# Last attention of a four-layer vision tower: order of the maxima, the results and the output projection within a step

## The reference, cut to what matters

```python
def gqa(x, wq, wk, wv, wo, n_kv):          # D_MODEL 128, N_HEADS 8, D_K 16
    B, S, _ = x.shape
    q = (x @ wq).reshape(B, S, N_HEADS, D_K).transpose(0, 2, 1, 3)
    k = (x @ wk).reshape(B, S, n_kv, D_K).transpose(0, 2, 1, 3)
    v = (x @ wv).reshape(B, S, n_kv, D_K).transpose(0, 2, 1, 3)
    k = jnp.repeat(k, N_HEADS // n_kv, axis=1)
    v = jnp.repeat(v, N_HEADS // n_kv, axis=1)
    scores = jnp.einsum('bhqd,bhkd->bhqk', q, k) / jnp.sqrt(jnp.float32(D_K))
    attn = jax.nn.softmax(scores, axis=-1)
    out = jnp.einsum('bhqk,bhkd->bhqd', attn, v)
    return out.transpose(0, 2, 1, 3).reshape(B, S, D_MODEL) @ wo

logits = jax.nn.relu(x.mean(axis=1) @ r_w1 + r_b1) @ r_w2 + r_b2
sel = jnp.argmax(jax.nn.softmax(logits, axis=-1), axis=-1)
for i, nkv in enumerate((8, 4, 1)):
    out = jnp.where((sel == i)[:, None, None], gqa(x, *params[i], nkv), out)
# x is the normalized h; the kernel's output is h + out
```

## Time and profile before

| what | us |
|---|---|
| median of 3 runs | 1234.58 |
| lowest and highest run | 1231.76, 1241.58 |
| the profiled execution's own time | 1236.1 |
| its span, first to last instruction | 1234.3 |
| PE busy (share of the span) | 1098.2 (89%) |
| DVE busy | 904.1 (73%) |
| ACT busy | 845.1 (68%) |
| POOL busy | 526.2 (43%) |

### The profile page before, as it was taken

How to read it: one execution, slowest core, us unless ns; L and a number is a source line. 1 busy time by engine, 2 the same in 40 slices (tenths; PEclk the granted TensorE clock), 3 DMA queues, 4 the chain that set the end, 5 groups by cost and what they waited for, 6 DMA issues and landing times. The chain is left out here.

```text
span 1234.3 us, 29279 instructions
## 1 busy us (share of the span) xinstructions
PE 1098.2 (89%) x8508; PEld 910.6 (74%) x8508; DVE 904.1 (73%) x2770; ACT 845.1 (68%) x2821; POOL 526.2 (43%) x885
## 2 busy tenths in 40 slices
PE   8999979999998999887388599998899899869996
PEld 5778857888887788776288477786678688657884
DVE  0488847999976889956565488886899788755774
ACT  1498858888885555557243378887788499846995
POOL 0379864444304278855252653323342011034552
PEclk9999989999999999988599689999999999959997
DMA  7300002322210000001522200000333100024441
GB/s 293 96 2 3 2 1 63 110 71 65 65 43 23 1 2 1 2 1 38 195 61 50 63 14 2 11 2 2 115 113 113 34 3 2 2 80 122 131 130 36
DMA packets 50824, 66.68 MB, mean 54 GB/s; under 512 B 8100, under 2 KB 30904, under 8 KB 50552
## 3 DMA queue, kind: packets, MB, share of 16 engines
q1 hardware_dynamic: 44552, 53.39, 14.2%
q0 software_dynamic: 4432, 6.59, 2.1%
q10 hardware_dynamic: 1696, 4.98, 1.0%
HBM read 58.32 MB, written 6.71 MB: 53 GB/s over the span
## 5 line engine op out<-in xcount | busy, mean ns | idle before, releaser
L495 DVE TENSOR_TENSOR f_parts<-T,f_parts 128x512 fp32r<-128x512 f32 (+1 forms) x240 | 181.7, 796 | 21.1 <-ACT f_parts L479 19.6
L471 ACT ACTIVATE T<-quad_bank,f_b1s 128x512 f32<-128x512 f32 (+1 forms) x240 | 150.5, 648 | 43.2 <-PE quad_bank L442 34.3
L442 PE MATMUL quad_bank<-XP,f_wp 128*128 128x512 f32 (+1 forms) x720 | 165.3, 373 | 1.1 <-ACT T L471 1.1
L442 PEld LDWEIGHTS quad_bank<-XP,f_wp 128*128 128x128 f32 x720 | 125.6, 188 | 26.4 <-ACT T L471 1.4
L479 ACT ACTIVATE f_parts<-T 128x512 fp32r<-128x512 f32 (+1 forms) x240 | 132.7, 593 | 0.0
L954 ACT ACTIVATE a_late<-quad_bank,a_shift 108x108 f32<-108x108 f32 x352 | 119.1, 363 | 2.7 <-DVE a_shift L1022 2.4
L455 PE MATMUL bank<-f_parts,f_wp 128*128 128x512 f32 (+1 forms) x480 | 116.7, 379 | 4.7 <-DVE XT L504 2.0
L455 PEld LDWEIGHTS bank<-f_parts,f_wp 128*128 128x128 f32 x480 | 85.4, 192 | 23.5 <-DVE a_late L524 2.8
L384 POOL TENSOR_TENSOR f_wp<-f_ws,const 128x512 fp32r<-128x512 f32 (+1 forms) x32 | 31.0, 968 | 122.3 <-DMA f_ws<-in_f_w 53.9
L954 ACT ACTIVATION_READ_ACCUMULATOR a_late<-quad_bank,a_shift 108x1 f32 x352 | 77.2, 219 | 0.0
L765 POOL TENSOR_TENSOR a_ve<-a_mv,const 108x1 f32<-108x1 f32 x44 | 8.3, 189 | 152.1 <-DVE a_mv L1079 152.0
(11 more groups left out here) (470 smaller groups left out, 3105.9 us busy)
## 6 DMA issues: line engine op xcount, KB each, us to landing
a_late<-f_gates SPq DMA_DIRECT2D x64, 256.0 KB, 3.2
a_wqk<-in_a_wqk SPq DMA_DIRECT2D x24, 256.0 KB, 2.5
f_ws<-in_f_w SPq DMA_DIRECT2D x16, 256.0 KB, 3.8
pats<-in_patches SPq DMA_DIRECT2D x5, 648.0 KB, 10.7
pats<-in_patches ACTq DMA_DIRECT2D x5, 648.0 KB, 14.8
a_late<-f_gates SPq DMA_DIRECT2D x16, 128.0 KB, 3.6
f_w1a<-in_f_w SPq DMA_DIRECT2D x1, 2048.0 KB, 11.4
f_w2a<-in_f_w SPq DMA_DIRECT2D x1, 2048.0 KB, 16.2
```

Of the source, the lines that this page charges most:

```text
L442: mm = pe.matmul(self.m.quad_bank[:, q % 4, 0:w], self.wp[0][:, e % 2, a, c * 128:(c + 1) * 128], self.xp[:, b, t0:t0 + w], start=((a, b) ...
L471: act.activation(self.full[:, q % 4, 0:w], self.m.quad_bank[:, q % 4, 0:w], self.func, bias=self.b1s[:, e * self.chunks + c:e * self.chunk ...
L495: dve.tensor_tensor(self.lo[:, q % self.ring, 0:w], self.full[:, q % 4, 0:w], self.hi[:, q % self.ring, 0:w], ALU.subtract).then_inc(self. ...
```

## The change

On TensorE, `probabilities(t - 2, par, 1)`, that is P1, moves from behind wo to ahead of it. On VectorE, recT and oT move from the end of step t (for group t-2) to step t+1 (there group t-3 of that step), where they stand between the two maxima: mx0, shift0, recT, oT, mx1, shift1. The waits and the operations themselves stay as they are.

```diff
@@ TensorE, step
                 if isinstance(t, int) and t == 2:
                     keep_busy(pe, m, obank, 3)
+                if on(t, 2):
+                    probabilities(t - 2, par, 1)
                 if on(t, 3):
                     g = t - 3
                     pe.wait_ge(o_done, g + 1)
...
                     pe.wait_ge(wo_loaded[q], landed(g, q))
                     pe.matmul(xbank[0:P, 0:D], oT[:, :], wo[:, q, :], start=True, stop=True).then_inc(y_psum, 1)
-                if on(t, 2):
-                    probabilities(t - 2, par, 1)
@@ VectorE, step
                 if on(t, 1):
                     maxima(t - 1, q, 0)
+                if on(t, 3):
+                    g = t - 3
+                    dve.wait_ge(o_psum, g + 1)
+                    at_least(dve, o_done, g)
+                    dve.tensor_copy(recT[:, :], z_at).then_inc(o_read, 1)
+                    dve.wait_ge(o_read, g + 1)
+                    at_least(dve, y_psum, g)
+                    dve.tensor_tensor(oT[:, :], o_at, recT[:, :], ALU.mult).then_inc(o_done, 1)
+                if on(t, 1):
                     maxima(t - 1, q, 1)
...
-                if on(t, 2):
-                    g = t - 2
-                    dve.wait_ge(o_psum, g + 1)
-                    at_least(dve, o_done, g)
-                    dve.tensor_copy(recT[:, :], z_at).then_inc(o_read, 1)
-                    dve.wait_ge(o_read, g + 1)
-                    at_least(dve, y_psum, g)
-                    dve.tensor_tensor(oT[:, :], o_at, recT[:, :], ALU.mult).then_inc(o_done, 1)
```

## The result

| | before | after |
|---|---|---|
| median of 20 runs, us | 1234.53 | 1240.71 |
| lowest and highest | 1228.32, 1241.58 | 1231.61, 1248.41 |
| ratio, 95% interval | | 1.0047 (1.003 to 1.0064) |
| profiled execution, its span | 1236.1, 1234.3 | 1246.6, 1244.8 |

What follows compares the result with a forecast made beforehand. PE was taken to bound the stage, with the order of work deciding. Loop +3.45, unrolled steps +0.65 and tail +1.2 sum to +5.3 us, giving a median of 1239.9 us, range 1234.5 to 1244.5.

Steps and rivals of the forecast that it cites:

- The point to see: Last attention, PE: wo stands exactly in the hole where P1 waits for ACT's pT0, and just covers that wait.
- E: Loop step behind the loop's branch; forecast hole ahead of P1 0.30 us, next S0 at 4.52.
- F: The other loop step, not behind the branch; forecast hole ahead of P1 0.26 us, its next S0 at 9.11.
- P1's wait: On PE, P1 starts 0.15 us behind pT0's end; lower end 0.05, which would make the whole change +3.3.
- A pair of 9.11: Two successive loop steps forecast at 9.11 us, for 8.665 before; loop +3.45 us.
- The ring: Cycle over PE and ACT: P1, wo, qk, v, v's copy, exps1, xT, pT0, P1; 4.48 us.
- part 2: DVE's recT and oT between the maxima: all fits barely, slack about 0 and 0.07 us, z at most 0.05 late.
- Rival C: Chance 0.20: DVE becomes the bound if the moved pair costs 0.2 us more; +7.7 us, 1242.3.
- Unrolled steps +0.65: The four unrolled steps t = 3 to 6 take 4.48 us each instead of 4.315, +0.65 us.
- Tail +1.2: At t = 24 wo stands behind P1, so h, recs, z and o come later at half clock: +1.2 us.
- Rival B: Chance 0.15: early maxima win, P1 finds pT0 ready at S1's end; faster, together -1.0 us, 1233.6.
- Rival D: Chance 0.02: PE's clock falls to half in the stage, with a hole each step; +60 us.

Runs made afterwards that it cites:

- exchanged banks: Changed kernel with P1 moved to x's PSUM bank, wo and v to P0's bank: ratio to before 1.002; the same with VectorE's old order: 0.9987.

## Why the prediction was right, and where it wasn't

**Sign, size and stage: right.** The stage's own loss is 4.03 us in the profiled executions. The median's +6.2 is above it, but the interval, from 3.7, holds it; what the rest is, beyond the scatter of the code ahead of the stage, stays open.

**"The point to see": right, and shown.** wo stood in the place of the hole. The hole of 0.30 in E came out as 0.30, that of 0.26 in F as 0.18; a filler in it costs 0.02 a step, and taking P1's wait away removes it.

**P1's wait, 0.15 taken with 0.05 as the lower end: right, with luck.** It is 0.15 where P1 does wait (1162.59 to 1162.74). But the row it was read from doesn't show it: in the kernel before P1 stands behind wo by wo's pitch of 0.30 to 0.31 in both steps, and in F that is 0.23 behind pT0's end. That it was 0.15 in E is a coincidence. The Trainium skill, "Advanced Engine Details and Errata", section Network/Comms, gives 50 to 100 ns for reading a semaphore; by that figure alone the hole in E would be 0.20 to 0.25, an estimate, and the trace shows 0.30.

**A pair of 9.11: measured 9.10, and that is luck, as errors cancel.** The two steps came out the other way round, E 4.59 for 4.52 and F 4.52 for 4.59. The step that failed is "I take P1 to wo as 0.37 and wo to qk as 0.31, each by its leader's pitch". The 0.31 was read where wo's weight load starts 0.01 ahead of its matmul (1172.61 and 1172.62 in the kernel before). In the kernel with TensorE's part alone it starts 0.09 ahead, qk follows wo by 0.22, and P1's own pitch is 0.39. The ring is shorter by 0.07 a step or so, and that kernel's pair is 9.00. The other 0.10 comes from part 2.

**Part 2, "all fits, barely": wrong.** oT's end was forecast at S0 + 2.22 and came at 2.21. But "in time for wo at 2.40" left out wo's weight load, which starts 0.23 behind oT's end, at S0 + 2.44. The matmul is at 2.45 then, 0.02 later behind P1 than without VectorE's part, but qk is 0.30 behind it and not 0.22. recs comes at S0 + 3.49 and z at 3.87, both 0.02 late. So VectorE's order adds 0.89 us to the loop on top of the hole. Rival C was right that the moved pair costs, and wrong on the way: in the changed kernel S0 stands 0.51 behind o, its pitch, and 0.15 behind the qk add's end, where 0.12 was forecast, and with exchanged banks it is the same; the ring closes over recs, z and o. Without the hole, VectorE's path is the bound and costs 2.41 by itself. Why the load starts 0.23 behind oT here and 0.14 in the kernel with exchanged banks stays open.

**Unrolled steps +0.65: measured +0.20.** They were charged by the loop's ring, 4.48 a step, and take 4.36. The same shorter pitch behind wo, 0.22 for 0.31, is most of the difference; the hole there is 0.13 to 0.15.

**Tail +1.2: the mechanism was right, the size 0.99 at half clock and 0.66 at full.** wo lasts 0.64 there, not the 0.76 taken, and z to o is 0.34, not 0.41. In the profiled execution little of it shows in the end time: from S0 at t = 23 to the last h it is 10.69 us against 10.36. The clock fell some 2 us of work later in that run (v, z and o of t = 23 ran at full clock), so that P1 of t = 24 stands 5.69 behind S0 of t = 23 and not 6.35, which gives 0.66 of the 0.99 back. That is luck of the run, as other executions with the same order show the full clock to o and beyond.

**The sum.** The parts in the profiled executions are 3.50, 0.20 and 0.33, together 4.03, for 3.45, 0.65 and 1.2. The ends of the range don't follow from its own recipe (1237.9 - 3 is 1234.9, 1242.3 + 3 is 1245.3); the measured time lies well inside either way.

**Rival B: refuted.** mx0 comes 0.22 earlier with respect to S0 (0.76 for 0.98) and nothing is gained: with VectorE's part alone the pair is 9.83, and with the exchanged banks, where P1 waits for nothing, the new VectorE order is 2.41 slower than the old. **Rival D** did not happen in the changed kernel, and it did in the one with VectorE's part alone. The Trainium skill's rule ("TensorE: Matmul & The Clock Gate", section Part 4: PE-mode transpose) that turning doesn't count as busy for the clock gate is neither shown nor refuted: the clock stayed at 1.00 with ten turned blocks and a hole in each step, and it fell behind a larger hole in a kernel with the same turned blocks.

## What to carry to other kernels

An instruction whose inputs are long ready can be what hides the wait of the one behind it. Before two neighbours on an in-order engine are exchanged, write down for each when its inputs are ready and when its slot comes; if the one that moves forward is ready only 0.1 us behind its new slot, the loss can be paid in each step, as the 0.18 and 0.30 were here. A result that another engine needs at once (oT for wo) should not be put behind work with slack; and where a place on an engine is idle anyway, as VectorE's between the qk add and mx0, the work that stands there is free, and moving it out delays what it is put ahead of: mx1 started 0.22 us later (S0 + 2.13 for 1.91).

## What was not expected of the hardware

- A wait against a constant passed 0.05 us behind the event (oT's end 1133.91, wo 1133.96). The same wait in the loop, with two more waits on register values behind it, passed 0.22 behind it (1183.65, 1183.87). In the kernel with exchanged banks, with as many waits on register values, it was 0.14 (1161.80, 1161.94), so their number alone doesn't set it. Writing the loop out cut the change's cost from 3.50 to 0.92 us. The runs don't separate the register waits from the other differences of the two forms.
- Turned blocks start 0.15 behind the event they wait for, in the loop and written out alike: P1 behind pT0, z behind recs (1164.42, 1164.57).
- How early a matmul's weight load can start shows in the pitch of the next matmul: wo to qk is 0.22 us with the load 0.09 ahead of wo's matmul (1156.19, 1156.28) and 0.30 with it 0.01 ahead (1163.14, 1163.15).
- Behind an idle stretch of 0.60 us, PE's granted clock was 0.52 and a step took 6.57 instead of 4.96 us, in 2 of the 8 steps that have such a stretch.
- Writing out sixteen steps did not cost anything in this stage: 68.88 against 69.32 us.
